# A two-layer attention block on one core: spread matmuls kept in float32 on half the rows, queries and exponentials left in PSUM, new load order and new order at the end

## The chip, the core and the metric

The kernel runs on one core of one Trainium2 chip. The metric is the device time of one execution in microseconds; three runs of the kernel before are shown. The engines are TensorE (PE, its weight loads PEld), VectorE (DVE), ScalarE (ACT), GpSimd (POOL) and SyncE (SP). Each works through its own instructions in the order in which the program has them, and they wait for one another through semaphores.

## What is computed

`x` is (8, 128, 16, 16) in float32. Two layers are added to it, each on a group-normalised input (groups of four channels):

```
x = x + L0(gn(x))      # 1x1 conv to q, k, v; 4 dilations (1, 2, 4, 8) of 32 channels, 2 heads each;
                       # per pixel a softmax over 9 shifted keys, sum of 9 shifted values,
                       # times a per-image gate = softmax(mean(gn(x)) @ w_gate.T + b_gate)
x = x + L1(gn(x))      # p = W_qkv x + b; 4 heads of 32 channels; att = softmax(p p^T / 16) over channels;
                       # W_proj (att p) + b_proj
```

## The kernel before

**Layout.** The eight images go in two phases of four (phase 0: images 0, 2, 4, 6; phase 1: 1, 3, 5, 7). Within a phase the partitions hold 4 images x 32 channels, so that one tile of 256 pixels serves one dilation `s` of four images. `project(n)` makes such a tile (kind 0 query, 1 key, 2 value) by four matmuls of 32 columns each, and ACT's `copy_tile(n)` brings it from PSUM to SBUF.

**First layer.** For each dilation and each column offset `ci`, DVE's `multiply_qk` multiplies queries with shifted keys (`qk`), and PE's `sum_scores` sums over channels; after a phase's four dilations the 9 scores of every pixel lie in 576 columns of one PSUM bank pair. `softmax_shift`, ACT's `softmax_exp` and `softmax_divide` give `prob` (the gate is multiplied in). Scores lie on 128 partitions as quarter of the picture `j` x 32 rows; `spread(ph, s, chunk)` brings the probabilities of three offsets back to the 128 channel partitions, by one selection matrix `sel[:, j, s]` for each quarter, into one of two PSUM areas; `multiply_pv` multiplies that with the shifted values (`pv`), and waits for it; the spread after next waits for the multiplication. So PE and DVE go in step, two areas deep. The nine products are summed in 8 additions per dilation: on POOL for phase 0 and for dilations 0 and 1 of phase 1, on DVE (`add_neighbours`) for dilations 2 and 3 of phase 1 (`POOL_SUMS = (ND, 2)`). `restore(g)` brings the sums of two images back to 128 channels in PSUM, `first_residual(g)` adds `x`.

In phase 1, dilations 1 to 3, the spread multiplies in bfloat16: ACT and DVE split `prob` in three bfloat16 parts (`first_part`, `split_rest`, `second_part`, `third_part`), and three matmuls are accumulated for each quarter.

**Second layer.** It goes in four groups `g` of two images: statistics (`squares`, `group_stats`, `second_variance`, POOL's `rsqrt`, `second_norm_bias`), normalisation, `project_second`, `copy_projection`, `transpose`, `copy_pT`, `attention`, `attention_shift`, `attention_exp`, `attention_divide` (a block-diagonal 128 x 128 matrix `ablk`), `fuse`, `copy_fused`, `finish`, `second_residual`, store. Groups 0 and 1 (phase 0) run beside phase 1 of the first layer; groups 2 and 3 are all that is left once the sums of phase 1 are there.

**Order.** There is no scheduler: each engine's order is the list of calls at the end of its block. `keep_clock(n)` is n matmuls whose result nobody reads.

## Time and profile before

| | |
|---|---|
| median of 3 runs | 90.77 us (89.9, 90.77, 91.79) |
| span of the profiled execution, first to last instruction | 88.6 us; the page gives no total of that execution, and the median lies 2.17 us above the span |
| DVE busy | 74.1 us, 84% |
| PE busy | 71.5 us, 81% (weight loads 55.5 us) |
| POOL busy | 45.6 us, 52% |
| ACT busy | 33.9 us, 38% |

A time beside an instruction in these views is its own duration; neighbours on one engine overlap by some 0.08 us, so the step from one to the next is that much shorter. One float32 matmul leaves two records, a bfloat16 one leaves one; the counts behind an x in rows of PE are records. The line of PE's matmuls is that of a helper (L818) for nearly all of them, and the tiles tell them apart: `xn` projections, `qk` sums of scores, `prob` or `part` spreads, `acc` restores, `xt` the matmuls of `keep_clock`.

### The profile page before, as it was taken

Reading aid. Unit: us, or ns where it says so; the run is one execution under the profiler, and the core shown is the slowest. Engines: PE = TensorE matmul, PEld = TensorE weight load, DVE = VectorE, ACT = ScalarE, POOL = GpSimd, SP = SyncE. Lnnn points to the kernel's source line nnn. Section 1 sums busy time; section 2 is a strip of 40 time slices with the busy share of each in tenths; the row PEclk is TensorE's granted clock in tenths of the full one; section 3 lists DMA queues with packets and bytes.
Section 4 is the critical chain, followed back from the end, with each engine's and each line's share of the span. In section 5 each row is a group of like instructions: output and inputs, shape, how many; then the busy total and the mean of one; then the engine's idle time right before and its main releaser. Section 6 shows DMA issues by size and latency. Waiting matters only on the chain.

```text
span 88.6 us, 2254 instructions
## 1 busy us (share of the span) xinstructions
PE 71.5 (81%) x896; PEld 55.5 (63%) x896; DVE 74.1 (84%) x193; ACT 33.9 (38%) x104; POOL 45.6 (52%) x82
## 2 busy tenths in 40 slices
PE   0299997999967899295998799995998098999970
PEld 0299784576425797193988677794876054766840
DVE  1278399999999969999699888999999959875990
ACT  4496699063650000000018333040695036367220
POOL 7404585068000199793999998699992000600000
PEclk9999999999999999999999999999999858999999
DMA  1992013000000000000000000000000000003145
GB/s 24 326 360 62 0 33 64 0 0 7 0 0 4 4 7 0 0 0 0 4 7 0 0 0 0 0 0 7 0 0 7 0 0 4 0 0 118 43 145 174
DMA packets 3019, 3.11 MB, mean 35 GB/s; under 512 B 320, under 2 KB 2752, under 8 KB 3008
## 3 DMA queue, kind: packets, MB, share of 16 engines
q1 hardware_dynamic: 2576, 2.69, 9.6%
q10 hardware_dynamic: 432, 0.26, 1.3%
q8 instruction: 7, 0.11, 0.6%
q14 instruction: 4, 0.03, 0.1%
HBM read 1.91 MB, written 1.05 MB: 33 GB/s over the span
## 4 chain that ended last, share of the span: by engine, by line
DVE 45%; PE 28%; POOL 12%; issue 5%; ACT 4%; DMA 4%; DVEq 0%; ACTq 0%
PE ps L818 27%; DVE qk L615 22%; DVE pv L665 10%; POOL pv L368 6%; POOL acc L368 6%; DMA xt<-x_dram 4%; DVE acc L677 3%; DVE pv L677 3%; DVE ssum L632 1%; PE ps L954 1%; DVE x L710 1%; ACT pT L445 1%; DVE acc L665 1%; DVE x L684 1%; DVE smax L622 1%
## 5 line engine op out<-in xcount | busy, mean ns | idle before, releaser
L818 PE MATMUL ps<-prob,sel 128*128 128x180 f32 (+6 forms) x120 | 18.7, 309 | 4.8 <-DVE pv L665 3.6
L818 PEld LDWEIGHTS ps<-prob,sel 128*128 128x128 f32 x120 | 17.0, 190 | 6.9 <-DVE pv L665 5.1
L615 DVE TENSOR_TENSOR qk<-q,k 128x128 f32<-128x128 f32 (+7 forms) x36 | 21.1, 650 | 0.1
L665 DVE TENSOR_TENSOR pv<-ps,v 128x128 f32<-128x128 f32 (+7 forms) x32 | 17.1, 568 | 2.4 <-PE ps L818 2.0
L368 POOL TENSOR_TENSOR pv<-pv 128x240 f32<-128x240 f32 (+3 forms) x24 | 16.2, 682 | 2.0 <-DVE pv L665 1.8
L818 PE MATMUL ps<-xn,wp 128*32 128x256 f32 (+1 forms) x208 | 16.4, 382 | 0.1
L368 POOL TENSOR_TENSOR acc<-acc,pv 128x256 f32<-128x256 f32 (+4 forms) x20 | 13.2, 664 | 0.5
L333 POOL TENSOR_TENSOR rstd<-gvar,mhalf 128x2 f32<-128x2 f32 (+1 forms) x6 | 4.9, 824 | 15.4 <-DVE gvar L563 15.3
L818 PEld LDWEIGHTS ps<-xn,wp 128*32 128x32 f32 (+1 forms) x208 | 9.8, 116 | 4.4 <-ACT xn L452 0.6
L423 ACT ACTIVATE expd<-shifted 128x576 f32<-128x576 f32 x2 | 1.4, 683 | 21.3 <-DVE shifted L625 21.3
L818 PE MATMUL ps<-xt 128*128 128x128 f32 x28 | 5.9, 382 | 3.9 <-DMA xt<-x_dram 3.9
L818 PE MATMUL ps<-qk,cs 128*32 128x192 f32 (+6 forms) x176 | 7.8, 302 | 1.2 <-ACT v L413 0.7
L818 PE MATMUL ps<-part,sel 128*128 128x168 bf16 (+5 forms) x108 | 7.0, 221 | 1.2 <-DVE pv L665 1.2
L818 PEld LDWEIGHTS ps<-xt 128*128 128x128 f32 x28 | 5.2, 281 | 3.9 <-DMA xt<-x_dram 3.9
L818 PEld LDWEIGHTS ps<-part,sel 128*128 128x128 bf16 x108 | 6.4, 98 | 1.8 <-DVE pv L665 1.8
L368 POOL TENSOR_TENSOR acc<-pv 128x256 f32<-128x256 f32 x4 | 2.9, 728 | 8.8 <-DVE pv L665 8.8
L818 PE MATMUL ps<-acc,cs 128*32 128x256 f32 x64 | 5.5, 488 | 2.2 <-DVE acc L677 2.0
L818 PEld LDWEIGHTS ps<-qk,cs 128*32 128x32 f32 x176 | 4.7, 110 | 3.8 <-ACT v L413 1.2
L445 ACT ACTIVATE pT<-x 128x256 f32<-128x256 f32 x8 | 3.3, 412 | 6.6 <-DVE x L684 6.6
L588 DVE TENSOR_REDUCE sums<-xt 128x1 f32<-128x256 f32 x8 | 2.9, 412 | 2.8 <-DMA xt<-x_dram 2.7
L818 PEld LDWEIGHTS ps<-acc,cs 128*32 128x32 f32 x64 | 2.4, 138 | 4.1 <-issue 3.3
L818 PE MATMUL ps<-p,mT 128*128 128x256 f32 x16 | 4.6, 399 | 0.3 <-ACT mT L472 0.2
(81 smaller groups left out, 104.2 us busy)
## 6 DMA issues: line engine op xcount, KB each, us to landing
xt<-x_dram SPq DMA_DIRECT2D x4, 256.0 KB, 3.5
out_dram<-x SPq DMA_DIRECT2D x8, 128.0 KB, 1.8
wp<-wpack_dram SPq DMA_DIRECT2D x1, 325.0 KB, 5.3
sel<-selc_dram SPq DMA_DIRECT2D x4, 64.0 KB, 3.9
cs<-consts_dram ACTq DMA_DIRECT2D x1, 130.0 KB, 3.5
cs<-consts_dram ACTq DMA_DIRECT2D x2, 64.0 KB, 2.6
```

The lines of the kernel that those rows point to most:

```text
L333: nc.gpsimd.tensor_tensor(rstd[:, bs], gvar[:, bs], mhalf[:, bs], ALU.pow).then_inc(rstd_ready, 1)
L368: nc.gpsimd.tensor_tensor(o, a, b, ALU.add).then_inc(added, 1)
L423: nc.scalar.activation(expd[:], shifted[:], ACT.Exp, scale=SCALE0).then_inc(exp_ready, 1)
L445: nc.scalar.activation(pT[:, g, 2 * i:2 * i + 2, :].rearrange("p t n -> p (t n)"), x1[:, b, :], ACT.Square, accum_out=sums1[:, b, 1:2]).th ...
L588: nc.vector.tensor_reduce(sums[:, b, 0:1], xt[:, b, :], AX.X, ALU.add).then_inc(sum_ready, 1)
L615: last = nc.vector.tensor_tensor(o, a, b, ALU.mult)
L622: link(nc.vector.tensor_reduce(smax[:], view(ps, 512 * SC[ph], [[1, QP], [256, 3], [QP, 3]]), AX.XY, ALU.max))
L632: link(nc.vector.tensor_reduce(ssum[:], view(expd, 0, [[1, QP], [QP, KK]]), AX.X, ALU.add))
L665: last = nc.vector.tensor_tensor(o, a, b, ALU.mult)
L677: nc.vector.tensor_tensor(o, a, b, ALU.add).then_inc(dve_added, 1)
L684: nc.vector.scalar_tensor_tensor(out=x1[:, b, :], in0=ps[:, BANK[g] + i, 0:N], scalar=1.0, in1=xt[:, b, :], op0=ALU.mult, op1=ALU.add, acc ...
L818: return nc.tensor.matmul(o, w, m, start=start, stop=stop)
```

## The change

1. **Loads.** Images 0, 4, 6 come one by one from SP's queue and image 2 from ACT's; then 1 and 3 together, the weights, 5 and 7. The constants move from ACT's queue to SP's, behind a wait.
2. **Start.** POOL makes `nbias` of the first layer itself, behind its power; DVE's first normalisation needs only `rstd` and takes three images (was two). The first key tile is projected first, its queries stay in PSUM, `first_variance(1)` stands behind the first `multiply_qk`. Queries of dilations 2 and 3 of phase 1 stay in PSUM too (`project_query`, in the bank of phase 0's scores). These are three of 24 tiles that ACT no longer copies.
3. **Softmax.** `softmax_exp` writes to PSUM; `softmax_divide` reads it there.
4. **Spread.** No bfloat16 parts; every spread is one float32 matmul per quarter on 64 rows (was 128), quarters in the order 0, 2, 1, 3.
5. **Sums.** Dilation 3 of phase 1 is summed by TensorE in PSUM (`sum_second`), but for two additions on DVE.
6. **Second layer.** `ablk` is replaced by `anorm` (64 columns, one instruction for a group) and four 32-row matmuls in `fuse`; some copies and one normalisation change engine, and the order of the last two groups changes.
7. **`keep_clock`.** 38 such matmuls in 14 places (before: 14 in 4).

```diff
-NORM_ON_ACT = (4, 6, 1, 3, 5, 7)
+NORM_ON_ACT = (4, 1, 3, 5, 7)
+X_PIECES = ((0,), (2,), (4,), (6,), (1, 3), (5, 7))
+Q_IN_PSUM = [(0, 0, 0)] + [(0, s, PHASES - 1) for s in range(2, ND)]
...
             for ph in range(PHASES):
-                rsqrt(ph, of_phase(ph))
+                bs = of_phase(ph)
+                rsqrt(ph, bs)
+                pool.wait_ge(rstd_ready, ph + 1)
+                nc.gpsimd.tensor_tensor(nbias[:, bs], gst[:, bs, 0], rstd[:, bs], ALU.mult).then_inc(nbias_ready, 1)
...
             def softmax_exp(ph):
-                nc.scalar.activation(expd[:], shifted[:], ACT.Exp, scale=SCALE0).then_inc(exp_ready, 1)
+                nc.scalar.activation(view(ps, 512 * SC[ph], [[1, KK * QP]]), shifted[:].rearrange("p k n -> p (k n)"),
+                                     ACT.Exp, scale=SCALE0).then_inc(exp_ready, 1)
...
+            def project_query(ph, s):
+                if ph:
+                    pe.wait_ge(prob_ready, 1)
+                for j in range(SLOTS):
+                    last = mm(view(ps, q_columns(s), [[1, N]], 32 * j, 32), wp[:, W_QKV + CD * s:W_QKV + CD * s + CD],
+                              xn[:, PHASES * j + ph, :])
+                last.then_inc(q_ready, 1)
...
-                for j in range(4):
+                for j in (0, 2, 1, 3):
                     i0, i1 = row_offsets(s, j)
                     dims = lambda slot, row: [[slot, i1 - i0], [row, QR], [1, c1 - c0]]
                     o = view(ps, 1024 * (c % 2) + 64 * QR * j + W * i0 + c0, dims(W, 64))
-                    for n in range(3 if split else 1):
-                        if split:
-                            w, m = sel16, view(part[n], (3 * ci + i0) * QP + c0, dims(QP, W))
-                        else:
-                            w, m = sel, view(prob, (ph * KK + 3 * ci + i0) * QP + c0, dims(QP, W))
-                        last = mm(o, w[:, j, s, :], m, start=(n == 0), stop=(n == 2 or not split))
+                    half = 64 * (j // 2)
+                    m = view(prob, (ph * KK + 3 * ci + i0) * QP + c0, dims(QP, W), half, 64)
+                    last = mm(o, sel[half:half + 64, j % 2, s, :], m)
...
+            def sum_second():
+                def tile(s, t, first, r0=0, r1=H, c0=0, c1=W, start=False, stop=False):
+                    dims = [[W, r1 - r0], [1, c1 - c0]]
+                    at = r0 * W + c0
+                    for j in range(SLOTS):
+                        rows = slice(32 * j, 32 * j + 32)
+                        last = mm(view(ps, 512 * (BANK[2] + j) + at, dims, 32 * s, 32), ident[rows, rows],
+                                  view(t, first + at, dims, 32 * j, 32), start=start, stop=stop)
+                        if stop and s == LAST_UNIT:
+                            last.then_inc(restored, 1)
+                pe.wait_ge(pv_ready, 12 * PHASES)
+                pe.wait_ge(added, ADDS * sum(POOL_SUMS))
+                pe.wait_ge(dve_added, ADDS)
+                for s in range(ND):
+                    tile(s, acc, (ND + s) * N, start=True, stop=s != LAST_UNIT)
+                s = LAST_UNIT
+                for slot in (3, 5, 1, 0, 2, 7):
+                    ci, ri = divmod(slot, 3)
+                    if slot == 7:
+                        pe.wait_ge(last_added, 2)
+                    tile(s, pv[s], slot * N, *valid_rows(s, ri), *columns(DIL[s], ci)[:2], stop=slot == 7)
```

**How the instructions stand, three places.** At the start of DVE's program (`sums` and `gst`, `gsq`, `gvar` are statistics, `xn` the normalised images, `qk` the first products), before:

```order
L588 TENSOR_REDUCE sums<-xt 128x1 x5
L560 TENSOR_TENSOR gst<-ps,signs 128x4x2
L562 TENSOR_TENSOR gsq<-gst 128x4
L563 SCALAR_TENSOR_TENSOR gvar<-gst,gsq 128x4
L588 TENSOR_REDUCE sums<-xt 128x1 x3
L569 TENSOR_TENSOR nbias<-gst,rstd 128x4
L592 TENSOR_SCALAR xn<-xt,rstd,nbias 128x256 x2
L560 TENSOR_TENSOR gst<-ps,signs 128x4x2
L562 TENSOR_TENSOR gsq<-gst 128x4
L563 SCALAR_TENSOR_TENSOR gvar<-gst,gsq 128x4
L569 TENSOR_TENSOR nbias<-gst,rstd 128x4
L615 TENSOR_TENSOR qk<-q,k 128x48x15
```

The same place in the changed kernel:

```order
L560 TENSOR_REDUCE sums<-xt 128x1 x4
L535 TENSOR_TENSOR gst<-ps,signs 128x4x2
L537 TENSOR_TENSOR gsq<-gst 128x4
L538 SCALAR_TENSOR_TENSOR gvar<-gst,gsq 128x4
L560 TENSOR_REDUCE sums<-xt 128x1 x2
L564 TENSOR_SCALAR xn<-xt,gst,rstd 128x256 x3
L560 TENSOR_REDUCE sums<-xt 128x1 x2
L591 TENSOR_TENSOR qk<-ps,k 128x48x15
L535 TENSOR_TENSOR gst<-ps,signs 128x4x2
L537 TENSOR_TENSOR gsq<-gst 128x4
L538 SCALAR_TENSOR_TENSOR gvar<-gst,gsq 128x4
L591 TENSOR_TENSOR qk<-ps,k 128x768
```

Both `nbias` are gone, and the second variance now stands behind the first product. On PE, from the dummies ahead of phase 1's spreads to the first `group_stats`, before:

```order
L818 MATMUL ps<-xt 128x128 x5
L818 MATMUL ps<-prob,sel 128x3x4x16 x4
L818 MATMUL ps<-prob,sel 128x3x4x15 x4
L818 MATMUL ps<-acc,cs 32x256 x8
L818 MATMUL ps<-prob,sel 128x3x4x15 x4
L818 MATMUL ps<-part,sel 128x3x4x16 x12
L818 MATMUL ps<-sums,cs 128x4
```

In the changed kernel:

```order
L805 MATMUL ps<-xt 128x128 x6
L805 MATMUL ps<-prob,sel 128x3x4x16 x4
L805 MATMUL ps<-prob,sel 128x3x4x15 x8
L805 MATMUL ps<-prob,sel 128x3x4x16 x4
L805 MATMUL ps<-acc,cs 32x256 x8
L805 MATMUL ps<-prob,sel 128x3x4x14 x4
L805 MATMUL ps<-sums,cs 128x4
```

The restore of group 0 stands two spreads later, and twelve bfloat16 matmuls are four in float32. On PE behind the last spreads, where phase 1 is restored, before:

```order
L818 MATMUL ps<-pT 32x32 x16
L818 MATMUL ps<-acc,cs 32x256 x16
L818 MATMUL ps<-wp,ablk 128x128
L818 MATMUL ps<-sums,cs 128x4
L818 MATMUL ps<-p,mT 128x256
L818 MATMUL ps<-sums,cs 128x4
L818 MATMUL ps<-wp,ablk 128x128 x3
```

In the changed kernel:

```order
L805 MATMUL ps<-acc,cs 32x256 x16
L805 MATMUL ps<-pv,cs 32x128 x8
L805 MATMUL ps<-pv,cs 32x16x8 x4
L805 MATMUL ps<-pv,cs 32x8x8 x8
L805 MATMUL ps<-pv,cs 32x16x8 x4
L805 MATMUL ps<-wp,anorm 32x128 x8
L805 MATMUL ps<-xt 128x128 x2
L805 MATMUL ps<-sums,cs 128x4
L805 MATMUL ps<-p,mT 128x256
L805 MATMUL ps<-xt 128x128 x2
L805 MATMUL ps<-sums,cs 128x4
```

The nine products of the last dilation (`pv`) enter here, six of them as matmuls of their own and the centre as part of `acc`; both fuses stand ahead of the statistics, and dummies between these.

## Rows read from the trace of the kernel before

**Rows 1.** The page: busy time of each engine; the chain that ended last.

```profile
PE 71.5 (81%) x896; PEld 55.5 (63%) x896; DVE 74.1 (84%) x193; ACT 33.9 (38%) x104; POOL 45.6 (52%) x82
DVE 45%; PE 28%; POOL 12%; issue 5%; ACT 4%; DMA 4%; DVEq 0%; ACTq 0%
```

**Rows 2.** Timeline to 11 us: start, us, engine, line, tiles, count, idle before.

```profile
6.17 2.48 PE L818 MATMUL ps<-xt 128*128 128x128 f32 x10
7.07 1.01 POOL L333 TENSOR_TENSOR rstd<-gvar,mhalf 128x4 f32<-128x4 f32 x1 [3.87 <-DVE gvar L563]
10.96 6.64 DVE L615 TENSOR_TENSOR qk<-q,k 128x720 f32<-128x720 f32 x10
```

**Rows 3.** Timeline from 12 to 22 us: the gate's inputs, and the key tile of phase 1.

```profile
12.00 0.80 POOL L342 TENSOR_TENSOR pooled<-pooled,nbias 128x8 f32<-128x8 f32 x1
12.87 1.71 POOL L345 COPY pexp<-pooled 128x128 f32<-128x128 f32 x2
14.63 0.61 PE L818 MATMUL ps<-wp,pexp 128*128 128x4 f32 x4 [0.24 <-POOL pexp L345]
15.72 1.18 PE L818 MATMUL ps<-qk,cs 128*32 128x384 f32 x16 [0.48 <-DMA cs<-consts_dram]
19.16 0.37 ACT L413 COPY k<-ps 128x256 f32<-128x256 f32 x1 [0.31 <-PE ps L818]
21.80 0.75 DVE L622 TENSOR_REDUCE smax<-ps 128x64 f32<-128x576 f32 x1
```

**Rows 4.** DVE's groups by shape, 23.2 to 26 us, POOL idle: count, busy, mean ns.

```profile
L632 DVE TENSOR_REDUCE ssum<-expd 128x64 f32<-128x576 f32 x1 | 1.1, 1142 | 0.0
```

**Rows 5.** The same, 10.9 to 22 us, POOL nearly idle.

```profile
L615 DVE TENSOR_TENSOR qk<-q,k 128x256 f32<-128x256 f32 x3 | 1.2, 413 | 0.0
L615 DVE TENSOR_TENSOR qk<-q,k 128x384 f32<-128x384 f32 x1 | 0.5, 544 | 0.0
```

**Rows 6.** The same, 32.9 to 36.5 us, while POOL adds; the last row is one multiply_pv.

```profile
L615 DVE TENSOR_TENSOR qk<-q,k 128x384 f32<-128x384 f32 x1 | 1.1, 1054 | 0.0
L665 DVE TENSOR_TENSOR pv<-ps,v 128x768 f32<-128x768 f32 x1 | 0.9, 943 | 0.0
```

**Rows 7.** DVE's timeline, 30 to 54 us.

```profile
32.97 3.44 DVE L615 TENSOR_TENSOR qk<-q,k 128x256 f32<-128x256 f32 x4
37.97 3.07 DVE L615 TENSOR_TENSOR qk<-q,k 128x128 f32<-128x128 f32 x6
48.95 0.82 DVE L635 SCALAR_TENSOR_TENSOR prob<-expd,gate,srec 128x576 f32<-128x576 f32 x1
53.47 0.75 DVE L646 TENSOR_TENSOR part<-rest,part 128x576 bf16<-128x576 f32 x1
```

**Rows 8.** PE's timeline: spreads of two chunks each, then the restore of group 0.

```profile
27.48 2.79 PE L818 MATMUL ps<-prob,sel 128*128 128x192 f32 x16 [0.56 <-DVE prob L635]
44.48 2.00 PE L818 MATMUL ps<-prob,sel 128*128 128x128 f32 x16
57.27 1.92 PE L818 MATMUL ps<-part,sel 128*128 128x168 bf16 x24
52.71 1.07 PE L818 MATMUL ps<-acc,cs 128*32 128x256 f32 x16
```

**Rows 9.** Windows: length, busy of PE, PEld, DVE, ACT, POOL (counts), then PEclk.

```profile
30.00:34.00 4.00, 3.64 (x24) 3.38 (x23) 3.23 (x5) 0.00 (x0) 3.27 (x5) 1.00 0.02 4
50.00:54.00 4.00, 3.90 (x34) 3.04 (x35) 3.23 (x5) 1.14 (x2) 3.63 (x8) 1.00 0.00 0
70.00:74.00 4.00, 3.32 (x33) 1.64 (x33) 2.95 (x16) 1.42 (x6) 0.00 (x0) 0.57 0.00 0
```

**Rows 10.** Timeline: first and last of dilation 3's eight additions, restores of phase 1.

```profile
69.03 0.28 DVE L677 TENSOR_TENSOR acc<-acc,pv 128x128 f32<-128x128 f32 x1
...
70.28 0.29 DVE L677 TENSOR_TENSOR acc<-acc,pv 128x128 f32<-128x128 f32 x1
70.68 3.33 PE L818 MATMUL ps<-acc,cs 128*32 128x256 f32 x32 [2.05 <-DVE acc L677]
```

More of the change, by code:

```diff
@@ L65 @@
 F32 = mybir.dt.float32
-BF16 = mybir.dt.bfloat16
 ALU = mybir.AluOpType
@@ L146, in build @@
         shifted = sb("shifted", [P, KK, QP])
-        expd = sb("expd", [P, KK, QP])
         prob = sb("prob", [P, PHASES, KK, QP])
-        part = [sb(f"part{n}", [P, KK, QP], BF16) for n in range(3)]
-        rest = sb("rest", [P, KK, QP])
-        sel16 = sb("sel16", [P, 4, ND, P], BF16)
         smax = sb("smax", [P, QP])
@@ L190, in build @@
         arec = sb("arec", [P, GROUPS, GB])
-        ablk = sb("ablk", [P, GROUPS, GB, P])
+        anorm = sb("anorm", [P, GROUPS, GB, HD1])
         mT = sb("mT", [P, GROUPS, GB, P])
@@ L231, in build @@
         prob_ready = sem("prob_ready")
-        part_ready = [sem(f"part{n}_ready") for n in range(3)]
-        rest_ready = sem("rest_ready")
-        sel16_ready = sem("sel16_ready")
         spread_ready = sem("spread_ready")
@@ L268, in build, with x_slice, piece_of @@
         for ph in range(PHASES):
-            tiles += [(kind, s, ph) for s in range(ND) for kind in (0, 1)] + [(2, s, ph) for s in range(ND)]
+            tiles += [(kind, s, ph) for s in range(ND) for kind in (0, 1) if (kind, s, ph) not in Q_IN_PSUM]
+            tiles += [(2, s, ph) for s in range(ND)]
+        def x_slice(i):
+            piece = X_PIECES[i]
+            return slice(piece[0], piece[-1] + 1, PHASES)
+        def piece_of(b):
+            return [b in piece for piece in X_PIECES].index(True)
+        LAST_UNIT = ND - 1
         def of_phase(ph):
@@ L748, in _ @@
                 multiply_qk(1, 1, i)
+            for i in range(2):
+                multiply_pv(0, 0, i)
             multiply_qk(1, 2, 0)
-            for i in range(3):
-                multiply_pv(0, 0, i)
+            multiply_pv(0, 0, 2)
             for i in range(1, 3):
@@ L801, in _ @@
                 norm(3, i)
-            for i in range(2):
-                second_residual(0, i)
+            copy_pT(2, 0)
+            second_residual(0, 0)
+            copy_pT(2, 1)
+            second_residual(0, 1)
             attention_shift(2)
@@ L901, in spread @@
                     pe.wait_ge(pv_ready, c - 1)
-                split = ph == PHASES - 1 and s > 0
-                if split and s == 1 and chunk == 0:
-                    pe.wait_ge(sel16_ready, ND - 1)
-                    for n in range(3):
-                        pe.wait_ge(part_ready[n], 1)
                 c0, c1, _ = columns(DIL[s], ci)
-                for j in range(4):
+                for j in (0, 2, 1, 3):
                     i0, i1 = row_offsets(s, j)
@@ L981, in _ @@
             first_stats(0)
-            keep_clock(5)
+            keep_clock(8)
+            project(0)
+            project_query(0, 0)
             first_stats(1)
-            for n in range(11):
+            for n in range(1, 10):
                 project(n)
@@ L1058, in _ @@
             attention(3)
+            finish(1, 1)
             for i in range(2):
                 fuse(2, i)
-            finish(1, 1)
             for i in range(2):
```

298 lines of the change are left out of this document (161 added, 137 removed).

## Prediction

> **What bounds the kernel now.** I read the page first: DVE is busy 84% of the span and leads the chain that ended last with 45%, PE 28%, POOL 12% [rows 1]. The timeline then gives the stages. To 10.96 us nothing but loads, statistics and the first tiles [rows 2]; from there DVE works nearly without a break, first at products alone, then at products in step with PE's spreads; around 52 us POOL and PE take over for a moment, since the restore of group 0 waits for POOL's 32 additions of phase 0 and starts at 52.71 [rows 8]; DVE's additions end at 70.6, PE's restore of phase 1 starts at 70.68 [rows 10], and a tail of 17.9 us to 88.6 is the second layer of the last two groups. I follow six milestones, A to F. Two facts decide the sizes between them. DVE is not merely busy, it is slowed: a product of 384 elements with both inputs in SBUF takes 544 ns with POOL idle [rows 5] and 1054 ns while POOL adds [rows 6]. And DVE waits for PE: in 30 to 34 us and 50 to 54 us it is busy 3.23 of 4 us [rows 9].
>
> **A, the first product (before 10.96).** In front of it now: POOL's power ends at 8.08 [rows 2], then come nbias on DVE, two normalisations on ACT and two on DVE beside them, and the tiles q and k, projected and copied one behind the other. The change takes nbias off DVE's way (an estimate of 0.2 for four numbers), puts the key first (one copy less, 0.37 [rows 3]) and puts one more normalisation on DVE (0.4 more, as 256 elements take [rows 5]). Against it, eight dummies stand ahead of the first projection; five took 2.48 us [rows 2], so eight take 4.0 at that rate, from about 6 us to 10 us, where five end at 8.65 now. Four loads of one image in two queues instead of two of two may give up to 0.4 us earlier data. I take 10.7, -0.3; ends 10.3 and 11.3.
>
> **B, the first key tile of phase 1 in use (before 20.1,** which is 21.80 less two products of 0.85 [rows 3]**).** This part costs. The second variance stood in an idle stretch of DVE; now it stands behind the first product. So POOL's second power (1.0, as the first [rows 2]) ends at about A + 0.9 + 0.5 + 1.1 = A + 2.5; before, it was through by A. Behind it come, on POOL, nbias (bounded by 0.2, a small operation with no wait, and 0.85, the step from 12.00 to 12.87 of linked ones [rows 3]; I take 0.5), three small operations (2.0, within three such steps) and pexp's 1.71: pexp is there at A + 6.7 = 17.4, where it was there at 14.6. PE's gate_logits waits for it, and behind gate_logits are queued the scores of dilations 0 and 1, v3, q0 and k0 of phase 1. From gate_logits' end at 15.24 to the end of the copy of k0 at 19.53 PE and ACT needed 4.3 us [rows 3], of which 0.48 was a wait for constants [rows 3] that will be there. So k0 arrives at 17.4 + 0.6 + 3.8 = 21.8. DVE, at the same work plus the variance (0.55), wants it at 10.7 + 9.15 + 0.55 = 20.4. It waits 1.4 us, and B comes at 21.8, +1.7. The end in the other direction is no wait, 20.4; in the bad one, 22.6. ACT's norms of phase 1 come later as well, by about 2 us, behind three copies; the copies that DVE needs next are still in time by 0.7 us.
>
> **C, prob of phase 0 (before 27.4,** when PE's first spread was let go [rows 8]**).** The nine-fold sum takes 1142 ns from SBUF [rows 4]; the maximum over as many elements of PSUM, with the same stride, takes 746 to 750 [rows 3]. I take the PSUM row: -0.39, each phase. The Trainium skill, "VectorE: DVE Perf Modes", section "The TRN2 errata — SBUF-src ops pay a fixed extra latency per instruction", says the opposite in its table: 58 cycles for an operation from SBUF, 120 from PSUM, so 0.065 us dearer. By the rule the two sums together would cost 0.13 where I book a gain of 0.78; the row of this case decides. C: 28.7, +1.3.
>
> **D, prob of phase 1 (before 49.77 [rows 7]).** Here lies most of the gain.
> - Ten products of phase 1's dilations 2 and 3 took 3.44 + 3.07 = 6.5 us of wall time while POOL added [rows 7]. A multiply_pv, with one input in PSUM, is not slowed: 768 elements take 943 ns in the same stretch [rows 6], 1.23 ns each, against 1.42 for 384 elements and 1.61 for 256 with POOL idle [rows 5]. With queries in PSUM the four of dilation 2 cost 4 x 0.46 and less the overlap 1.5, the six of dilation 3 2 x 0.34 + 4 x 0.2 = 1.5. Gain 3.5.
> - Waits for spreads in this part: 0.77 in 30 to 34 us [rows 9] and about the same again. They go if spreads get faster. A chunk now takes 1.40 us (2.79 for two) at 192 columns and 1.00 at 64 to 128 [rows 8], some 14 us for the twelve of a phase. On 64 rows, quarters 0 and 2 lie on different halves of the array and in different banks. No row shows two halves at once; the nearest one is the restore, four column strips of 32 at once: 8 matmuls of 256 columns in 1.07, 134 ns each, where a spread's of 192 columns takes 349 [rows 8], a factor of 3.5 per column out of 4. Bounds: no gain (14) and a half (7). I take 7.4, 0.62 a chunk, nearest to that row.
> - PE's work between C and D is then 7.4, the scores of three dilations 2.7, two queries 1.0 and 13 dummies 3.5 = 14.6 of some 18.3. It fits, with small waits; I book 0.5 for waits at the first chunks, where queries and three dummies stand between spreads, and 0.3 later.
> - The second nine-fold sum, -0.39.
>
> So -3.5 - 1.5 + 0.8 - 0.4 + 0.5 (a product of dilation 2 that comes in later) = -4.1, and D is 49.8 + 1.3 - 4.1 = 47.0, -2.8. POOL gains too, since the lock works both ways; its phase 0 is then through before it is waited for.
>
> **E, PE can start summing phase 1 (before 70.68).** Gone from DVE: the split, 0.75 [rows 7] and one like it, 1.5; the 0.77 idle in 50 to 54 us [rows 9], waits for the parts and for the restore, which stood behind POOL and now stands behind two more chunks; six of eight additions, at 1.5 us for the eight from 69.03 to 70.57 [rows 10] 1.1. Sum -3.4. Back come a wait of 0.4 for the first spread, which no split covers now, and 0.4 for waits at small chunks, whose bfloat16 matmuls were cheap; at the large ones float32 on half the rows takes 0.7 where bfloat16 took 0.96 (1.92 for two [rows 8]). sum_second also waits for POOL: 16 additions of phase 1 at 0.65 (3.27 us busy with 5 [rows 9]) to 0.8 and two powers of 1.0 are 12.4 to 14.8, from about 50.5 on, so 63 to 65.3, just not later than DVE. E is 70.7 - 2.8 - 2.6 = 65.3, -5.4.
>
> **F, the tail (before 17.9 us).** The 16 restores took 3.33 at half clock (mean 0.57 in 70 to 74 us [rows 9, 10]), because PE had idled two us. sum_second has 40 matmuls, 896 columns in a row for dilation 3; at the rate of the restore about 2 us warm, 3.5 cold, most of it before the last additions, and all four images appear at once, so DVE's four residuals run through: -0.6. Against it the last statistics stand behind finish(0, 0), DVE's copy for it and four dummies: +0.4. One anorm for two ablk, copies shared between DVE and ACT: -0.2 in the last chain. The tail is -0.4 to 0; E and F give 88.6 - 5.6 = 83.0.
>
> The median before lies 2.2 above the span, so **85.2 us**, a ratio of 0.94. A measurement of this kernel tells some 2% from no change (its three runs spread by that much).
>
> **Rivals.**
> 1. *The weights bound the spread.* At 64 columns a chunk takes as long as its 8 weight loads let it, 2.00 for the 16 of two chunks [rows 8], 125 ns each. If the loads of the two halves do not overlap, no chunk falls below 1.0: 12 us a phase, not 7.4. PE then has 19.2 of work between C and D where DVE has 18.3 with its waits (+1.0), and some 19.6 to E for 18.3 (+1.4). 87.6. The Trainium skill, "TensorE: Matmul & The Clock Gate", section "LDWEIGHTS (loading the stationary operand)", speaks for this one: a load of 32 rows takes as long as one of 128, the 128 columns count. Its section "Measured speedup vs the span model" speaks against it, with 3.07 times for four row tiles of 512 columns; no run here shows either.
> 2. *The halves run one behind the other (slower).* Then the twelve chunks stay at 14 us, the bfloat16 ones of phase 1 (0.96 for the large) become 1.0 to 1.25, and the dummies and queries come on top: 21.3 against 18.3 to D, 21.7 against 18.3 to E, which is 3.0 and 3.4 more, 91.6, and up to 93 with more waits at phase 1's small chunks. It decides as soon as a chunk takes more than about 1.0. Against it speaks the restore's factor of 3.5; it is of column strips, though.
> 3. *The gate does not hold DVE.* If POOL's small operations run at their short price and the loads come 0.4 earlier, the 1.4 us at B go: 84.0.
> 4. *The slow products are not POOL's doing.* Then the 3.5 do not come: 88.7, no change that can be told. Against: the same line at the same shape takes half as long with POOL idle [rows 5, 6].
>
> **Chances.** My forecast 0.57, its own range 83.5 to 87.0; rival 1 0.15; rival 2 0.08; rival 3 0.10; rival 4 0.05; the rest, such as a colder clock from the many short gaps, 0.05 around 89. The range reaches from 83.0 to 89.0; outside it are rival 2 and a little on either side. Faster by over 2% is below 88.95: all of the forecast and rival 3, most of 1, half of 4: 0.84. Slower by over 2%, above 92.6: 0.04. Between: 0.12.
>
> **What would show it.** Products of dilations 2 and 3 of phase 1 at 0.28 to 0.55 us each beside a busy POOL; the nine-fold sum at 0.75; two chunks at 192 columns in about 1.5 us instead of 2.79; k0 of phase 1 copied at about 21.8 with DVE idle before it; sum_second starting at 65 and needing 2 us at full clock. If two chunks take 2.0 us whatever their columns it is rival 1; if 2.8, rival 2. I would be wrong altogether if moving work onto PE made PE the bound in both phases.

## The result, and the profile after

| | median (range) | executions |
|---|---|---|
| kernel before | 90.84 us (89.9 to 91.79) | 4 |
| changed kernel | 86.08 us (84.63 to 87.42) | 4 |
| ratio | 0.940, 95% interval 0.927 to 0.953 | |

Two of the changed kernel's four executions have a mean granted clock of 0.98 and take 87.3 and 87.4 us, two have 0.995 and take 84.6 and 84.9; the ratio is made from the second kind, the traced execution is of the first. I put the traced one first, since its milestones can be read, and then ask where the further 2.5 us come from.

On the page of the changed kernel DVE is busy for 67.4 us where it was 74.1, PE for 73.3 where it was 71.5 [rows 1]; DVE still has the largest share of the chain that ended last, 39% where it had 45%. The clock row has a dip at a quarter of the span:

```profile
PE 73.3 (86%) x1004; PEld 52.3 (61%) x1004; DVE 67.4 (79%) x183; ACT 29.5 (34%) x92; POOL 40.7 (48%) x84
PEclk9999999995699999999999999999999999999999
DVE 39%; PE 34%; POOL 11%; issue 5%; DMA 5%; ACT 3%; SPq 1%; DVEq 0%; POOLq 0%
```

Its timeline to 13 us, beside rows 2 (start, us, engine, line, tiles, count, idle before and what ended it):

```profile
5.62 0.42 DVE L560 TENSOR_REDUCE sums<-xt 128x1 f32<-128x256 f32 x1 [1.13 <-DMA xt<-x_dram]
6.27 0.56 PE L805 MATMUL ps<-sums,cs 128*128 128x8 f32 x2 [0.83 <-ACT xn L392]
6.68 3.76 PE L805 MATMUL ps<-xt 128*128 128x128 f32 x16
10.38 1.94 PE L805 MATMUL ps<-xn,wp 128*32 128x256 f32 x16
12.45 0.91 DVE L591 TENSOR_TENSOR qk<-ps,k 128x720 f32<-128x720 f32 x1 [2.10 <-PE ps L805]
```

The last image of the first half lands at 5.6; the eight dummies run until 10.4, although the normalised inputs are there at about 9.7; and the 16 records of projections behind them take 1.94 us, 121 ns each. The first product starts at 12.45, where it started at 10.96 before [rows 2].

From 15 to 25 us, beside rows 3, and PE's clock there (length, busy time of PE, PEld, DVE, ACT, POOL with counts, then PEclk):

```profile
17.28 1.16 POOL L346 COPY pexp<-pooled 128x128 f32<-128x128 f32 x2
18.49 0.61 PE L805 MATMUL ps<-wp,pexp 128*128 128x4 f32 x4 [0.78 <-POOL pexp L346]
20.61 1.95 PE L805 MATMUL ps<-xn,wp 128*32 128x256 f32 x16
24.55 1.78 DVE L591 TENSOR_TENSOR qk<-q,k 128x720 f32<-128x720 f32 x2 [2.41 <-ACT k L412]
```

```profile
16.00:20.00 4.00, 2.58 (x31) 1.29 (x35) 3.93 (x11) 3.20 (x10) 2.29 (x4) 0.93 0.00 0
20.00:24.00 4.00, 4.00 (x64) 2.60 (x60) 2.14 (x9) 0.95 (x3) 2.38 (x7) 0.65 0.00 0
```

PE waits for the gate's input, is busy 2.58 of 4 us, and then the granted clock falls, to a mean of 0.65 over 20 to 24 us. Sixteen records of projections take 1.95 us there, where 16 took 1.07 before the dip (at 16.64), and DVE waits 2.41 us for the key tile.

Between prob of the two phases, beside rows 4, 7 and 8:

```profile
29.29 0.75 DVE L608 TENSOR_REDUCE ssum<-ps 128x64 f32<-128x576 f32 x1
...
36.81 1.51 DVE L591 TENSOR_TENSOR qk<-ps,k 128x256 f32<-128x256 f32 x4
39.87 1.54 DVE L591 TENSOR_TENSOR qk<-ps,k 128x128 f32<-128x128 f32 x6
...
44.26 1.11 PE L805 MATMUL ps<-prob,sel 64*128 64x128 f32 x16
...
48.33 0.82 DVE L611 SCALAR_TENSOR_TENSOR prob<-ps,gate,srec 128x576 f32<-128x576 f32 x1
...
49.20 1.53 PE L805 MATMUL ps<-prob,sel 64*128 64x192 f32 x16 [0.30 <-DVE prob L611]
```

The ten products that took 3.44 and 3.07 take 1.51 and 1.54; the nine-fold sum takes 0.75 instead of 1.14; two large chunks 1.53 instead of 2.79, two small ones 1.11 instead of 2.00. And at the end, beside rows 10:

```profile
67.60 0.73 PE L805 MATMUL ps<-acc,cs 32*32 32x256 f32 x32
68.15 1.41 PE L805 MATMUL ps<-pv,cs 32*32 32x128 f32 x48
69.44 0.42 DVE L663 SCALAR_TENSOR_TENSOR x<-ps,xt 128x256 f32<-128x256 f32 x1
```

The whole sum takes 2.0 us on PE, without a wait and at full clock, where the restore alone took 3.33.

The milestones, with the control and two of the experiments below:

| | forecast | changed | changed again | gate later | gate later, loads as before |
|---|---|---|---|---|---|
| A first product | 10.7 | 12.45 | 12.1 | 11.7 | 10.4 |
| B phase 1's key in use | 21.8 | 24.55 | 24.2 | 20.9 | 19.6 |
| C prob of phase 0 | 28.7 | 31.5 | 31.1 | 28.2 | 26.9 |
| D prob of phase 1 | 47.0 | 49.15 | 48.8 | 45.9 | 44.6 |
| E PE sums phase 1 | 65.3 | 67.6 | 67.2 | 64.35 | 63.0 |
| span | 83.0 | 85.6 | 85.2 | 82.4 | 81.1 |

(With the gate later, phase 1's key is no longer waited for; B is then the end of the products before it.) From C on the stages agree in all of them, C to D 17.7 us, D to E 18.45, E to the end 18.0, against 18.3, 18.3 and 17.7 forecast. What the traced execution has over the forecast stands in front of B.

Both traces of the changed kernel are of executions with the dip. What one without it looks like can be read from four experiments below that leave everything up to B as it is (queries copied, spreads on 128 rows, exponentials in SBUF, no dummies in the gaps) and whose traces have no dip there: A is 11.3 to 11.6, B 21.7 to 22.0. The changed kernel's own spans without a dip are 82.8 to 83.5. The same two stretches of PE's timeline, from the run with queries copied:

```profile
10.09 1.07 PE L805 MATMUL ps<-xn,wp 128*32 128x256 f32 x16
...
18.86 1.05 PE L805 MATMUL ps<-xn,wp 128*32 128x256 f32 x16
```

So the 2.5 us have two parts. About 0.8 us lie in the first projections, which take 1.07 us here and 1.94 above, and 1.65 between A and B: that is 10.4 us in all four, and 12.1 in all four traces with the dip (the changed kernel twice, quarters in order, the last unit summed by DVE). B of 21.7 to 22.0 and the stages behind it, 61.05 us, give 82.8 to 83.1, which are three of the four spans without a dip, so the whole difference lies in front of B.

### The profile page after: what moved, and what is told of

Its sections match the earlier page's. It is cut to its first block, busy times and chain, and to the rows that moved or that the text cites. A ratio compares the mean times of both kernels' runs of the same rounds, so it can differ in the third digit from the quotient of the medians.

```text
span 85.6 us, 2451 instructions
## 1 busy us (share of the span) xinstructions
PE 73.3 (86%) x1004; PEld 52.3 (61%) x1004; DVE 67.4 (79%) x183; ACT 29.5 (34%) x92; POOL 40.7 (48%) x84
## 3 DMA queue, kind: packets, MB, share of 16 engines
HBM read 1.84 MB, written 1.05 MB: 34 GB/s over the span
## 4 chain that ended last, share of the span: by engine, by line
DVE 39%; PE 34%; POOL 11%; issue 5%; DMA 5%; ACT 3%; SPq 1%; DVEq 0%; POOLq 0%
PE ps L805 33%; DVE pv L632 11%; DVE qk L591 9%; DMA xt<-x_dram 5%; POOL rstd L332 3%; POOL acc L369 3%; DVE acc L644 2%; DVE pv L644 2%; DVE x L663 2%; DVE prob L611 2%; DVE smax L598 2%; DVE ssum L608 2%; POOL pv L369 2%; DVE acc L632 1%; POOL pexp L346 1%
## 5 line engine op out<-in xcount | busy, mean ns | idle before, releaser
L805 PE MATMUL ps<-prob,sel 64*128 64x192 f32 (+6 forms) x192 | 17.8, 313 | 2.0 <-DVE pv L632 1.6
L805 PE MATMUL ps<-xn,wp 128*32 128x256 f32 (+1 forms) x208 | 18.5, 422 | 0.8 <-ACT q L409 0.7
L805 PE MATMUL ps<-xt 128*128 128x128 f32 x76 | 14.6, 338 | 3.4 <-DMA xt<-x_dram 3.4
L805 PEld LDWEIGHTS ps<-prob,sel 64*128 64x128 f32 x192 | 13.6, 186 | 6.1 <-DVE pv L632 3.5
L805 PEld LDWEIGHTS ps<-xt 128*128 128x128 f32 x76 | 12.2, 235 | 5.4 <-DMA xt<-x_dram 3.4
L591 DVE TENSOR_TENSOR qk<-q,k 128x672 f32<-128x672 f32 (+7 forms) x21 | 11.5, 606 | 2.4 <-ACT k L412 2.4
L369 POOL TENSOR_TENSOR acc<-pv 128x256 f32<-128x256 f32 x4 | 2.9, 725 | 10.9 <-DVE pv L632 10.9
L591 DVE TENSOR_TENSOR qk<-ps,k 128x128 f32<-128x128 f32 (+6 forms) x15 | 6.4, 485 | 2.1 <-PE ps L805 2.1
L428 ACT ACTIVATE pT<-x 128x256 f32<-128x256 f32 x8 | 3.3, 408 | 10.1 <-DVE x L663 10.1
L805 PEld LDWEIGHTS ps<-sums,cs 128*128 128x128 f32 x12 | 2.1, 225 | 3.8 <-issue 1.9
L412 ACT COPY k<-ps 128x256 f32<-128x256 f32 x8 | 3.0, 371 | 3.9 <-PE ps L805 3.7
L695 DVE SCALAR_TENSOR_TENSOR x<-ps,wp,x 128x256 f32<-128x256 f32 x8 | 3.7, 480 | 0.7 <-PE ps L805 0.7
(81 smaller groups left out, 89.9 us busy)
```

Source lines behind the costliest of these rows:

```text
L369: nc.gpsimd.tensor_tensor(o, a, b, ALU.add).then_inc(added, 1)
L412: nc.scalar.copy(dst, src.rearrange("p (r c) -> p r c", c=W)).then_inc(proj_copied, 1)
L428: nc.scalar.activation(pT[:, g, 2 * i:2 * i + 2, :].rearrange("p t n -> p (t n)"), x1[:, b, :], ACT.Square, accum_out=sums1[:, b, 1:2]).th ...
L591: last = nc.vector.tensor_tensor(o, a, b, ALU.mult)
L695: nc.vector.scalar_tensor_tensor(out=x1[:, b, :], in0=ps[:, BANK[g] + i, 0:N], scalar=wp[:, W_BP:W_BP + 1], in1=x1[:, b, :], op0=ALU.add, ...
L805: return nc.tensor.matmul(o, w, m, start=start, stop=stop)
```

## Experiments

**The changed kernel again**, no edit. The runs with queries copied, with spreads on 128 rows and the first with the later gate are of the same chip. Quarters in order, exponentials in SBUF, the last unit summed by DVE and no gap dummies ran on another chip, without the changed kernel beside them; the kernel before, at a clock of 1.0, takes 89.4 to 89.8 us on the first chip, and three of four times 89.7 to 89.75 on the second, so differences of some tenths between the two sets carry that much doubt.

> The changed kernel as it is, the control for the three others. Span 83 to 85.6 us. The theory of the prediction says that DVE idles 1 to 2.5 us before the first key tile of phase 1, about 24.5 us into the profile seen. A second theory, for executions of this kernel that differ by 2.5 us: TensorE's clock falls to 1.2 GHz in 19 to 23.5 us in some and not in others; then the short ones show a granted clock of 1.00 there and the whole difference lies before 25 us.

86.17 us (84.61 to 87.25, 4 runs), ratio 0.940 (0.928 to 0.952). Two executions at a mean clock of 0.98 take 87.0 and 87.3, two at 0.996 and 1.0 take 85.3 and 84.6. Below, "the control" is 84.6 to 85.3, and another kernel's executions are set against it where their clock is as high.

**Queries copied to SBUF again**, that is the tiles of dilations 2 and 3 of phase 1.

```diff
-Q_IN_PSUM = [(0, 0, 0)] + [(0, s, PHASES - 1) for s in range(2, ND)]
+Q_IN_PSUM = [(0, 0, 0)]
...
-            for n in range(10, 17):
+            for n in range(10, 19):
                 copy_tile(n)
...
-            for i in range(2, ND):
-                project_query(1, i)
```

> Undoes one part: the queries of dilations 2 and 3 of phase 1 go through ACT to SBUF again, so that their ten products have two inputs in SBUF while GpSimd adds. If the shared reading with GpSimd is the cost that the prediction took it for, the ten products take about 6.5 us of wall time instead of 3.0, and the time is 2.5 to 3.5 us above the control (less what the two query projections and waits for spreads give back). If the products were slow for another reason (their shape, or the state of that program), they stay at 0.28 to 0.55 us each and the time moves by under 0.5 us.

89.82 us (88.71 to 91.59), ratio 0.984 (0.972 to 0.996); the two best, 88.7 and 89.1, are 4.0 above the control's mean, where I had expected 2.5 to 3.5. No execution of it has a clock above 0.98: in the traced one the clock falls to 0.51 in 44 to 46 us, behind waits of PE for DVE of 1.90 and 1.58 us. Its timeline of DVE:

```profile
32.08 1.23 DVE L591 TENSOR_TENSOR qk<-q,k 128x192 f32<-128x192 f32 x2
34.04 3.40 DVE L591 TENSOR_TENSOR qk<-q,k 128x256 f32<-128x256 f32 x4
39.00 3.06 DVE L591 TENSOR_TENSOR qk<-q,k 128x128 f32<-128x128 f32 x6
```

The twelve products take 7.7 us instead of 0.71 + 1.51 + 1.54 = 3.8: 3.9 us, nearly the whole difference (two waits of DVE for PE, 0.31 and 0.30 us where the clock is low, come on top, and a wait of 0.33 for a spread is gone). One input in PSUM takes the slowdown away. That it is POOL's doing can be read in the same trace, since POOL pauses among these products:

```profile
39.20 0.78 DVE L591 TENSOR_TENSOR qk<-q,k 128x128 f32<-128x128 f32 x1
41.59 0.48 DVE L591 TENSOR_TENSOR qk<-q,k 128x128 f32<-128x128 f32 x2
```

```profile
39.16 0.68 POOL L369 TENSOR_TENSOR pv<-pv 128x224 f32<-128x224 f32 x1
40.53 0.85 POOL L369 TENSOR_TENSOR pv<-pv 128x224 f32<-128x224 f32 x1
42.91 0.68 POOL L369 TENSOR_TENSOR pv<-pv 128x224 f32<-128x224 f32 x1 [1.53 <-DVE pv L632]
```

A product of 128 elements takes 0.78 us beside POOL's addition, and two of them 0.48 while POOL is idle. Rival 4 is out. Taking this one row of constants back costs 4.0 us, where the whole change gained 4.6 to 5.4 (4.6 between executions at a clock of 1.0 or near it, 0.06 of 90.8 by the ratio). Such prices don't add up: the next experiment costs more than the whole gain by itself.

**Spreads on all 128 rows**, as before: the selection has four quarters again and each matmul reads all rows of prob.

```diff
-sel = sb("sel", [P, 2, ND, P])
+sel = sb("sel", [P, 4, ND, P])
...
-for j in (0, 2, 1, 3):
+for j in range(4):
...
-half = 64 * (j // 2)
-m = view(prob, (ph * KK + 3 * ci + i0) * QP + c0, dims(QP, W), half, 64)
-last = mm(o, sel[half:half + 64, j % 2, s, :], m)
+m = view(prob, (ph * KK + 3 * ci + i0) * QP + c0, dims(QP, W))
+last = mm(o, sel[:, j, s, :], m)
```

> Undoes one part: each spread matmul runs on 128 rows again, four selection matrices, quarters in order. If the halves of the array work beside one another, as the forecast has it, two chunks of 192 columns take 2.8 us here instead of 1.53, the twelve chunks of a phase about 14 us instead of 8.3, and the time is 5 to 7 us above the control (near the kernel before, 91). If the weight loads had been the bound, the small chunks (64 to 96 columns) would take the same here as in the control, and the time would be 2 to 3 us above it.

90.73 us (90.44 to 93.01, 10 runs), ratio 1.008 (1.003 to 1.013): 5.8 above the control, and no faster than the kernel before. Its timeline of PE, and DVE's waits (us in total, times, longest):

```profile
44.43 2.00 PE L805 MATMUL ps<-prob,sel 128*128 128x128 f32 x16
...
49.35 5.46 PE L805 MATMUL ps<-prob,sel 128*128 128x192 f32 x32
```

```profile
DVE pv L632 <- PE ps L805: 5.9, 9, 1.4
```

A large chunk takes 1.37 on all rows (5.46 for four) and 0.77 on half of them (1.53 for two); a small one 1.0 and 0.55. The changed kernel's row of that wait says 0.8 us, 3 times. That is a factor of 1.8, also at the small chunks, where rival 1 had its weight loads as a floor. It could still come from a matmul on half the rows being cheaper by itself. PE's groups in a window of 0.3 us, first this run's, then the changed kernel's, say no (count, busy, mean ns of one):

```profile
L805 PE MATMUL ps<-prob,sel 128*128 128x192 f32 x4 | 0.9, 352 | 0.0
L805 PE MATMUL ps<-prob,sel 64*128 64x192 f32 x8 | 0.9, 349 | 0.3 <-DVE prob L611 0.3
```

One takes as long on 64 rows as on 128, 349 and 352 ns, but eight of them fit where four did: the halves overlap, and rivals 1 and 2 are out. Rival 2's price is about what this run pays: C to D is 20.65 us here and D to E 21.6, 3.0 and 3.1 more than in the changed kernel, where the rival said 3.0 and 3.4. The Trainium skill, "TensorE: Matmul & The Clock Gate", section "LDWEIGHTS (loading the stationary operand)", says that the rows of a load don't matter. The traces agree for one load, 190 ns on 128 rows and 187 on 64, but loads of two halves do not queue up as loads of the whole array do.

**Quarters in their own order**: 0, 1, 2, 3 instead of 0, 2, 1, 3, so that neighbours in the queue lie on the same half.

```diff
-for j in (0, 2, 1, 3):
+for j in range(4):
```

> The changed kernel with the quarters of each spread in the order 0, 1, 2, 3, still on 64 rows each, so that neighbours in the program share their half of the array (0 and 1 the upper, 2 and 3 the lower) and their PSUM bank. If two halves overlap only where neighbouring matmuls lie on different halves, two chunks of 192 columns take 2.3 to 2.8 us instead of 1.53 and the time is 3 to 6 us above the control. If it is enough that fewer rows are loaded, they stay near 1.5 us and the time within 0.5.

87.49 us; three of four executions at a clock of 0.98 took 87.5 to 87.7 and the fourth, at 1.0, 84.95, inside the control. Its timeline:

```profile
49.23 1.64 PE L805 MATMUL ps<-prob,sel 64*128 64x192 f32 x16 [0.30 <-DVE prob L611]
```

1.64 for two chunks against 1.53: the order is worth some 0.05 us a chunk, not the factor. The time goes as the expectation's second branch said, but for another reason than fewer rows: in the first chunk eight records of 349 ns again fit into 0.9 us, so the halves overlap although neighbours in the program share one.

**Exponentials in SBUF** and the nine-fold sum from there, as before.

```diff
+if ph:
+    act.wait_ge(prob_ready, ph)
-nc.scalar.activation(view(ps, 512 * SC[ph], ...), shifted, ACT.Exp, scale=SCALE0)
+nc.scalar.activation(expd[:], shifted[:], ACT.Exp, scale=SCALE0)
-nc.vector.tensor_reduce(ssum[:], view(ps, 512 * SC[ph], [[1, QP], [QP, KK]]), ...)
+nc.vector.tensor_reduce(ssum[:], view(expd, 0, [[1, QP], [QP, KK]]), ...)
```

> Undoes one part: the exponentials go to SBUF again and are summed and divided from there. If the nine-fold sum is dear because it reads SBUF with that stride, it takes 1.14 us instead of 0.75, both phases, and the time is 0.8 us above the control. By the rule that an operand in PSUM costs more, the sum would take 0.69 us and the time fall by 0.1.

87.01 us (85.55 to 88.42), ratio 0.949 (0.937 to 0.962); its two executions at full clock, 85.55 and 85.95, are 0.8 above the control's mean.

```profile
26.61 1.16 DVE L610 TENSOR_REDUCE ssum<-expd 128x64 f32<-128x576 f32 x1
...
44.70 1.14 DVE L610 TENSOR_REDUCE ssum<-expd 128x64 f32<-128x576 f32 x1
```

0.4 us dearer each time. The Trainium skill, "VectorE: DVE Perf Modes", section "The TRN2 errata — SBUF-src ops pay a fixed extra latency per instruction", has PSUM as the dearer source in its table; for this strided sum the trace says the opposite, 0.4 against the table's 0.065.

**Last unit summed by DVE** as before: eight additions, then 16 matmuls that restore the four images.

```diff
-add_last_column()
+add_neighbours(1, 3)
...
-for s in range(ND):
-    tile(s, acc, (ND + s) * N, start=True, stop=s != LAST_UNIT)
...
+last = mm(ps[32 * s:32 * s + 32, BANK[g] + i, 0:N], ident[:, at:at + 32], acc[:, 1, s, :])
```

> Undoes one part: dilation 3 of phase 1 is summed by eight additions on DVE again, and sixteen restores on 128 rows stand where sum_second stood. The prediction booked 1.1 us for six additions and 0.6 for the residuals that run through. Then the stretch from the last first-layer product to the end of the last residual is 1.5 to 2 us longer and the time 1.2 to 2 us above the control; more, 2.5 to 3.5, if TensorE's idle stretch of two us brings its clock down again as in the kernel before. If the tail is bound by the statistics and GpSimd's powers instead, the time rises by under 0.8.

85.75 us (85.26 to 89.7, 5 runs), ratio 0.948 (0.938 to 0.957). The four executions at full clock have a mean of 85.6, the control's two 84.96, those of the first comparison 84.8: the sum on PE is worth 0.6 to 0.8 us, where I had given it 1.2 to 2. The traced execution is the fifth; in it the restore waits for the additions, and the clock fell there as well as in the gate's gap:

```profile
68.79 2.74 PE L805 MATMUL ps<-acc,cs 128*32 128x256 f32 x32 [1.54 <-DVE acc L644]
```

That wait, 1.54 us, is absent from the changed kernel; the kernel before had 2.05 there and a clock of 0.57 behind it [rows 9, 10].

**No dummies in the gaps**: the four and eight at the start stay, all `keep_clock` behind the first projection go, 26 matmuls in 12 places, of which four are shown.

```diff
-            keep_clock(3, ST)
...
-            keep_clock(2, 3)
...
-            keep_clock(6)
...
-            keep_clock(2, BANK[1] + 1)
```

> The changed kernel without the twelve groups of dummies in gaps; the two groups before the first projection stay. If they do what their name says, the clock falls to 1.2 GHz somewhere behind 28 us in most executions and the time is 1 to 3 us above the control. If the matmuls of the kernel alone hold the clock, the time is the same or up to 0.5 us less, since 26 dummies (some 7 us of TensorE) no longer stand ahead of spreads and statistics; the waits of DVE for spreads at 34 us and of the statistics at 71 us get shorter.

86.21 us (85.8 to 87.79), ratio 0.953 (0.943 to 0.962). Its windows, then PE's timeline:

```profile
46.00:50.00 4.00, 3.56 (x22) 3.18 (x24) 2.40 (x5) 0.00 (x0) 3.84 (x11) 0.50 0.00 0
```

```profile
46.44 5.42 PE L805 MATMUL ps<-prob,sel 64*128 64x192 f32 x32 [1.84 <-DVE prob L611]
```

PE idles 1.84 us in front of phase 1's spreads, the clock is at 1.2 GHz from there, and four chunks take 5.42, where two take 1.53 in the changed kernel: 1.2 us lost in the end. Dummies pay, at least in this gap.

**The gate later.** PE's `gate_logits` moves behind the scores of dilation 0 and 1 and the projections of v3, q0 and k0 of phase 1 (behind `project(13)`); DVE's `gate_shift` into phase 1's first products, ACT's `gate_exp` behind the copy of tile 13.

```diff
             for n in range(1, 10):
                 project(n)
-            gate_logits()
             sum_scores(0, 0)
...
             project(13)
+            gate_logits()
...
             for i in range(2):
                 multiply_qk(1, 0, i)
+            gate_shift()
             softmax_shift(0)
```

> One step changed against the changed kernel: the gate's logits stand behind the projection of the first key tile of phase 1 on PE, its shift behind the first two products of phase 1 on DVE, its exponential behind four more copies on ACT. If GpSimd's late gate chain is what holds DVE, as milestone B of the prediction has it, DVE's wait of 2.4 us before the first product of phase 1 falls to under 0.5 and the time is 1.2 to 2.4 us below the control. If DVE is held there by PE's own work (projections and scores at half clock) the wait stays over 1.5 us and the time moves by under 0.5.

84.03 us (83.81 to 84.36, 4 runs), ratio 0.929 (0.921 to 0.938). Every execution has a clock of 0.998 or 1.0. Its page, and DVE's timeline:

```profile
PEclk9999999999999999999999999999999999999999
```

```profile
14.68 7.92 DVE L593 TENSOR_TENSOR qk<-q,k 128x672 f32<-128x672 f32 x17
```

17 products run through, with no wait for the key; PE is busy all of 16 to 20 us. The wait and, where it comes, the dip behind the gate's gap go with the place of `gate_logits`. It is 2.1 below the median of the changed kernel and 0.9 below the executions of it without a dip.

**Second set, on one chip: the later gate again, with five first dummies, with the old loads, with few dummies.**

> The kernel with the later gate once more, so that the three below have it on their own chip. 84.0 (83.8 to 84.4), the first product at 11.7, no drop of the granted clock between 18 and 24 us.

84.19 us (83.52 to 84.69, 6 runs). The traced execution, 84.65, has its first product at 12.2 and not at 11.7, since its first projections take 1.94 us where they took 1.38; the clock doesn't fall behind them.

Five dummies ahead of the first projection instead of eight:

```diff
-keep_clock(8)
+keep_clock(5)
```

> The later gate, with five dummies ahead of the first projection instead of eight. If the dummies hold the first product, as the forecast said (eight at 2.48 us for five end after the normalised inputs are there): the first projection starts at 9.7 instead of 10.2, the first product at 11.3 instead of 11.7, and the time falls by 0.3 to 0.5. Rival: the inputs hold it, and it stays within 0.1 with the dummies gone from PE's row. A third way: with fewer dummies the clock is still low when the projections begin, they take longer, and the first product is no earlier or later.

83.67 us (83.27 to 83.96, 6 runs), ratio 0.929 (0.924 to 0.934): 0.5 less. The first projections start at 8.5 and not at 10.1, and take 2.47 us for 1.94: they are slow, as the expectation's third way has it, and yet the first product starts earlier, at 11.1. But the loads of this execution landed earlier too (the statistics stood at 5.6, not 6.0), so the trace alone doesn't share it out.

The images in pairs, (0, 2), (4, 6), (1, 3), (5, 7), all from SyncE, then the weights; eight dummies.

```diff
-X_PIECES = ((0,), (2,), (4,), (6,), (1, 3), (5, 7))
+X_PIECES = ((0, 2), (4, 6), (1, 3), (5, 7))
...
-            load_x(0)
-            load_x(2)
-            load_x(3)
-            load_x(4)
+            for i in range(4):
+                load_x(i)
             sp.dma_start(wp[:], wpack).then_inc(w_loaded, 16)
-            load_x(5)
...
-            bs = x_slice(1)
-            act.dma_start(xt[:, bs, :], xv[:, bs, :]).then_inc(x_loaded[1], 16)
```

> The later gate, with the images loaded in pairs, 0 and 2, 4 and 6, then the second half's, all from SyncE's queue, as in the kernel before; the constants stay where the change put them. The forecast gave the new order up to 0.4 us of earlier data: then the first statistics and the first product come 0.2 to 0.4 later here, 84.3. Rival: four single loads in two queues win nothing, since all share the same engines, and the last image of the first half lands no later in pairs: within 0.2 of 84.0, or below it.

83.01 us (82.85 to 83.3, 6 runs), ratio 0.922 (0.917 to 0.927): the best of all, 1.2 below the same kernel with the new order of loads, and its spread is 0.45 us. My expectation had the sign right only in its rival. Its timeline:

```profile
3.97 1.40 DVE L557 TENSOR_REDUCE sums<-xt 128x1 f32<-128x256 f32 x4 [2.70 <-DMA xt<-x_dram]
5.78 0.53 PE L802 MATMUL ps<-sums,cs 128*128 128x8 f32 x2
6.16 2.98 PE L802 MATMUL ps<-xt 128*128 128x128 f32 x16
9.07 1.21 PE L802 MATMUL ps<-xn,wp 128*32 128x256 f32 x16
10.39 0.91 DVE L588 TENSOR_TENSOR qk<-ps,k 128x720 f32<-128x720 f32 x1 [0.56 <-ACT k L407]
```

The first image comes 0.6 later than in the changed kernel (DVE starts at 3.97 against 3.41), but the fourth is there when DVE comes to it, against 5.6. PE has no idle time between its two rows of dummies, the second runs faster, and the projections take 1.21 us, not 1.94.

The five first dummies, the new loads, and no dummies inside the spreads (seven in phase 0, three in phase 1); the eleven ahead of the scores and spreads and those of the tail stay.

> The later gate and five first dummies; gone as well are the dummies inside the spreads (seven in phase 0, three in phase 1). The three ahead of the first scores of phase 1, the two behind them, the six ahead of phase 1's spreads and those of the tail stay. If PE bounds 55 to 64 us, where it works without a gap, the 1.2 us of dummies there come back: 1.0 below the run with five dummies alone. Rival: with them gone the granted clock falls somewhere behind 50 us, as it did without any, and 0.5 or more of it is lost again, or the time goes up. Without both, DVE bounds it and it stays within 0.3.

83.67 us (83.12 to 84.9, 6 runs), ratio 0.928 (0.922 to 0.934), the same as with them, and the clock holds but for one execution at 0.979. The 1.2 us that three of these dummies took of PE between 55 and 58 us did not come back: A to E is 52.4 us against 52.65, so the expectation of 1.0 less missed. PE's waits, total, times and longest, say where they went:

```profile
PE ps L807 <- DVE pv L634: 4.2, 7, 1.3
```

With the dummies the same row is 1.6 us, 3 times: PE waits for DVE in their place, and for ScalarE's normalisation (0.49 us at 57.76). These ten cost nothing that can be told, and give nothing but, perhaps, the one execution of six in which the clock dips.

## Why the prediction was right, and where its steps failed

**The sum and its parts.** 85.2 us was forecast, 86.1 measured as the median, 84.6 to 84.9 in the executions without a dip of the clock. The span of 83.0 that the stages add up to is that of these executions, 82.8 to 83.5. From B on the stages were right, the two large gains among them; in front of B two errors cancel where the clock holds (A comes 0.6 to 0.9 late, and A to B is 0.7 shorter than forecast, so that B is 21.7 to 22.0 for 21.8). That the sum is so near is in that part luck. What comes on top of the span is 1.7 to 1.9 us in every execution whose span is on record, not 2.2: the 2.2 set the median of three executions against the span of one. And the kernel before has a dip of its own: beside the control it takes 89.4 to 89.8 in the four executions at a clock of 1.0, and 90.3 to 91.0 in the eight at 0.98. The trace that the forecast starts from has a clock of 0.981, its slow restores of 3.33 us included. Between executions that keep the clock the change is worth 4.6 us, not the 5.6 that were booked.

**A, forecast 10.7, measured 12.45 and 12.1, and 11.3 to 11.6 where the clock holds behind it: the step that failed.** It had two terms. "May give up to 0.4 us earlier data" had the wrong sign: with the loads as before A is 1.3 to 1.8 earlier (10.4 against 11.7 and 12.2 of the two runs with the later gate), and the kernel 1.2 us faster. For the dummies I said 4.0 us, and that they would end at 10; they took 3.76 and ended at 10.4. What I left out is that the projections behind them can go at the slow pace as well: 1.94 and 1.88 us in the two traces of the changed kernel, 1.07 to 1.19 in the four of the same head without a dip. Of the 2.06 us by which 12.45 lies behind 10.39, 0.49 is the statistics that start later (6.27 for 5.78), 0.78 the dummies' longer run (3.76 for 2.98), 0.73 the projections. I looked at when data came first, and the statistics wait for the image that comes last. Why the fourth single load lands later than the second pair isn't shown; SyncE issues one load in 0.45 us, so it is issued 0.45 later, and more of the traffic beside it is other data, but no run takes these apart.

**B, the gate's chain, forecast A + 11.1 with a wait of 1.4.** The chain is right in kind and, where the clock holds, too long: with queries copied and with no gap dummies, B is A + 10.4 and the wait 0.73. POOL's nbias took 0.20 where I took 0.5, pexp came at A + 6.0 where I said 6.7. That shorter chain hides A's error in the sum. But with the dip B is A + 12.1 and the wait 2.4. I had the row that could have warned me, a clock of 0.57 behind a gap of 2 us [rows 9, 10], and used it for the tail alone. A drop has to be reckoned with behind each new gap of PE: I named the gap in front of `gate_logits` and priced only DVE's side of it. What decides whether it comes isn't shown. PE's waits around it are alike in both kinds, 0.70 to 0.86 and 0.78 us with the dip, 0.84 and 0.78 without; what differs is the pace of the first projections before, 1.84 to 1.94 us in the four traces with the dip and 1.07 to 1.19 in the four without. Rival 3, the gate doesn't hold DVE, was not what happened, but as an edit (the later gate) it was worth 0.9 to 2.1 us.

**C.** B to C is 6.9 us, as forecast. The nine-fold sum is 0.39 cheaper each phase as booked, confirmed by the row in both kernels and by 0.8 us in the run with exponentials in SBUF.

**D, forecast 18.3 us behind C, measured 17.7.** The contended products: 3.5 forecast, 3.5 by rows 7 against the rows after (6.5 less 3.05), 3.9 by the experiment, which has two more of them. The two rows were forecast at 1.5 each and came out at 1.51 and 1.54. The spread: a chunk forecast at 0.62, measured 0.77 large and 0.55 small, 9.0 us for the twelve by their rows and not 7.4. The bound by the restore's factor of 3.5 was too hopeful for two halves, 1.8 is what they give; it cost nothing, since PE still keeps ahead (the remaining waits of DVE for it are 0.8 us in the whole kernel). That is also why the danger of rivals 1 and 2 was real: at 1.0 to 1.37 a chunk, as in the run on 128 rows, DVE waits 5.9 us and the gain is gone.

**E, forecast 18.3 behind D, measured 18.45.** Right within 0.2; sum_second is not late for POOL.

**F, forecast 17.7, measured 18.0.** The sum takes 2.0 us as forecast, and DVE's four residuals run through, 69.44 to 70.8. Of the -1.1 for six additions and -0.6 for the residuals, 1.7 together, the experiment finds 0.6 to 0.8; which of the two was too large, no run takes apart.

**The rivals.** 1, 2 and 4 are excluded by experiments; the "colder clock from the many short gaps", 0.05 in my chances, is what happened in half of the executions, but behind one place, the two waits of 0.7 to 0.9 us on either side of PE's last work before `gate_logits`.

## What to carry to other kernels

A wait on one engine has two prices: who waits behind it, and, on PE, what the clock may do to the matmuls after it. Where a stage begins with a reduction over several loads, order and group the loads for the one that lands last. Two inputs in SBUF on DVE beside a busy POOL can cost twice the time, and moving one of them to PSUM is a small edit; look for it first.
